# Second weights resident in SBUF, and a new hand-over to the second stretch of a mixture-of-experts kernel

## The chip, the cores and the metric

One core of one Trainium2 chip runs the whole program. The metric is the device time of one execution in microseconds (us). Engines are named TensorE (PE in the views; PEld is its weight load), VectorE (DVE), ScalarE (ACT), GpSimd (POOL) and SyncE (SP, which issues most DMA transfers).

## What is computed

Two transformer blocks with adaptive layer norm over 8 batches of 256 tokens of width 256. Block 0: causal softmax attention with 16 heads of 128, then a dense mixture of 8 experts (top 2). Block 1: linear attention, then a mixture of 16 experts of which each token takes 4. The change touches the last part and what runs beside it:

```python
    t = xf * rsqrt(mean(xf * xf) + EPS) * norm_w
    logits = t @ gate_w.T + gate_b
    vals, idx = top_k(logits, 4)
    gates_k = softmax(vals)
    G[m, idx] = gates_k
    h = einsum('mh,eoh->emo', t, w1) + b1
    a, b = minimum(h[..., ::2], 7.0), clip(h[..., 1::2], -7.0, 7.0)
    act = a * sigmoid(1.702 * a) * (b + 1.0)
    y = einsum('emi,edi->emd', act, w2) + b2
    delta = einsum('me,emd->md', G, y)
...
    x = x + gb * delta
```

## The kernel before

**Two tables of work.** Every engine runs its own list of stages. A planner (Plan.run, with a cost for each stage and a landing time for each transfer) merges chains of stages into these lists for the first part of the program. For the last part the lists are written by a loop by hand (lines 478 to 511). Semaphores hold every dependence, so the order alone is at stake.

**Routing and sending.** For batch b, f_gate gives the gate's logits, f_rank and f_pos the row of each (token, choice) in the DRAM tensor xsD, sorted by expert, and f_send scatters the tokens there: 8 indirect DMAs of 128 rows per batch on GpSimd (line 1905), all 8 on one semaphore of b % 4. f_gain and f_x (GpSimd, lines 1892 and 1897) make the batch's own output, which store writes to `out` (SyncE, line 840).

**Blocks.** 79 blocks of 128 sorted rows each belong to one expert; the expert's number stands in a table in SBUF (bi in the views), from which engines load it into a register. Block n runs through: xb (SyncE, line 810: its rows, 264 KB), w2x (SyncE, line 819: second weights of its expert, 256 KB, into a ring of four), w_in (ScalarE, line 1349: first weights, resident, times the norm's weight, two instructions), x_t and x_out (TensorE line 1073, ScalarE line 1356: rows transposed), h_mm (TensorE, line 1084: 8 calls, 16 instructions in the views), e_a, e_b, e_tanh, e_g, e_act (VectorE lines 1765, 1772, 1780, 1785, ScalarE line 1362: the gated activation), y_mm (TensorE, line 1093: 2 calls, 4 instructions), y_out (VectorE, line 1793) into a ring of five, YB: for n % 5 of 0, 1, 2 it shows as BC, 3 as RB, 4 as X, and tok and y_add (GpSimd, lines 1924 and 1934): an indirect DMA that adds the rows to `out` or, every second block, to accD. y_add n waits until y_add n-2 has landed. At the end merge (line 1941) adds accD to `out`.

**Two stretches.** Blocks 0 to 21 (FIRST = 22) hold the tokens of batches 0 to 4 and run beside the later batches; the planner sets their place. Blocks 22 to 78 hold the rest. Their rows can be loaded once every send of batch 7 has landed. Their xb ring has 11 places, and xb runs 8 blocks ahead. On SyncE they begin behind store 7 (lo is 22, ahead is 8, load_block adds xb n):

```python
    for n in range(lo, lo + ahead):
        load_block(n)
    for n in range(lo, lo + 2):
        p.add("w2x", n, slot=n % 4, by=16)
```

In the second stretch a turn of the loop puts on TensorE x_t n+1, h_mm n, y_mm n-2, and on ScalarE w_in n+1, x_out n+1, e_tanh n. The y product reads its weights from the ring W2 behind the wait for w2x:

```python
                on.wait_ge(*done("e_act", n))
                on.wait_ge(*done("w2x", n))
```

## Time and profile before

| | us |
|---|---|
| median of 3 runs | 1038.34 (1037.41 to 1038.93) |
| the profiled execution | 1038.5 |
| its span in the trace | 1036.2 |
| TensorE busy | 968.4 (93%) |
| VectorE busy | 725.9 (70%) |
| ScalarE busy | 673.3 (65%) |
| GpSimd busy | 427.6 (41%) |
| DMA traffic | 180.53 MB, mean 174 GB/s |
| granted TensorE clock, mean | 0.977 |

The profiled execution is one of the program; the page of its profile gives busy times and a chain of the work that ended last, of which TensorE holds 82%. The averages hide stages with different limits, so the rows below are read by stretch. An indirect DMA or a register load shows in a timeline on the engine that issues it; a bracket behind a row holds the idle time of that engine ahead of it and what ended it.

### The profile page before, as it was taken

The page shows a single profiled execution, that of the slowest core. Times are in us where ns is not written, and L with a number is a line of the kernel's source. Part 1 is how long each engine was busy: PE and PEld are TensorE (multiplying, and loading weights), DVE is VectorE, ACT ScalarE, POOL GpSimd, SP SyncE. Part 2 cuts the span into 40 slices and gives each one's busy share as a digit, 9 for nine tenths or more (in the row PEclk, how much of TensorE's full clock was granted, in tenths as well). Part 3 has the DMA queues.
Part 4 walks back from the last instruction along what each step waited for, and adds up shares of the span by engine and source line. Part 5 has one row for each costly group of instructions (what it writes and reads, how often), then busy time and mean ns, then how long its engine had stood idle before and what let it go on. Part 6 is the DMA issues. An engine that isn't in the chain of part 4 may idle for free.

```text
span 1036.2 us, 20508 instructions
## 1 busy us (share of the span) xinstructions
PE 968.4 (93%) x6020; PEld 821.6 (79%) x6020; DVE 725.9 (70%) x2545; ACT 673.3 (65%) x1944; POOL 427.6 (41%) x450
## 2 busy tenths in 40 slices
PE   7999999999999999999999999996879879999990
PEld 4769878888988887887888788885767769999980
DVE  3564656777767687777669677865888668888880
ACT  2657767668677767768767876782746347777650
POOL 3322421421461362255146136323165645666573
PEclk9999999999999999999999999998999899999995
DMA  9926992994799520020011004237268788899954
GB/s 307 306 84 223 375 375 88 338 377 145 278 358 379 179 84 1 22 94 22 1 67 70 2 12 163 66 133 277 53 163 185 203 221 217 223 226 225 227 120 81
DMA packets 93725, 180.53 MB, mean 174 GB/s; under 512 B 9949, under 2 KB 29085, under 8 KB 92717
## 3 DMA queue, kind: packets, MB, share of 16 engines
q1 hardware_dynamic: 73467, 148.55, 43.3%
q0 software_dynamic: 18800, 30.30, 13.1%
q8 instruction: 48, 0.79, 0.3%
q14 instruction: 64, 0.52, 0.2%
q10 hardware_dynamic: 1346, 0.36, 0.2%
HBM read 77.71 MB, written 107.99 MB: 179 GB/s over the span
## 4 chain that ended last, share of the span: by engine, by line
PE 82%; DVE 7%; issue 3%; DMA 2%; POOL 2%; ACT 1%; DVEq 0%; ACTq 0%; SPq 0%; POOLq 0%
PE bank L1084 12%; PE bank L1048 10%; PE bank L1020 10%; PE bank L1093 6%; PE bank L1038 5%; PE bank L1010 5%; PE bank L999 4%; PE bank L970 3%; PE bank L876 3%; PE bank L1039 2%; PE bank L885 2%; PE bank L1029 2%; PE bank L1009 2%; PE bank L954 2%; PE bank L992 2%
## 5 line engine op out<-in xcount | busy, mean ns | idle before, releaser
L1879 POOL TENSOR_TENSOR RB<-RB 128x512 f32<-128x512 f32 x64 | 66.7, 1042 | 277.3 <-DVE RB L1658 277.1
L1084 PE MATMUL bank<-RB 128*128 128x128 f32 x1264 | 158.1, 279 | 4.3 <-DVE BC L1772 1.7
L1084 PEld LDWEIGHTS bank<-RB 128*128 128x128 f32 x1264 | 151.3, 195 | 6.9 <-DVE BC L1772 2.3
L1349 ACT ACTIVATE RB<-RA,nw 128x512 f32 x158 | 105.4, 715 | 45.9 <-issue 18.7
L1048 PE MATMUL bank<-RA,RB 128*128 128x256 f32 x512 | 132.5, 381 | 0.3 <-issue 0.3
L1020 PE MATMUL bank<-RA 128*128 128x256 f32 x512 | 121.3, 380 | 0.0
L1020 PEld LDWEIGHTS bank<-RA 128*128 128x128 f32 x512 | 94.7, 190 | 15.0 <-issue 3.3
L1048 PEld LDWEIGHTS bank<-RA,RB 128*128 128x128 f32 x512 | 91.3, 190 | 13.6 <-issue 2.5
L1855 POOL TENSOR_TENSOR qs<-qs,half 128x4 f32<-128x4 f32 x64 | 65.6, 1025 | 63.6 <-DVE qs L1667 56.0
L1093 PE MATMUL bank<-RB,BC 128*128 128x256 f32 x316 | 83.7, 389 | 7.8 <-DVE BC L1785 7.0
L1250 ACT ACTIVATE RB<-bank 128x256 f32<-128x256 f32 x128 | 48.7, 380 | 45.7 <-PE bank L1039 43.1
L1038 PE MATMUL bank<-RB,RA 128*128 128x256 f32 x256 | 77.1, 383 | 0.0
L1905 POOL DMA_INDIRECT xsD<-SC,pu x64 | 65.7, 1026 | 27.2 <-issue 14.2
L1010 PE MATMUL bank<-RA 128*128 128x256 f32 x256 | 76.5, 380 | 0.0
L1658 DVE COPY RB<-bank 128x512 f32<-128x512 f32 x64 | 44.2, 690 | 44.3 <-PE bank L1020 43.9
L1231 ACT ACTIVATE RB<-bank 128x384 f32<-128x384 f32 x128 | 62.0, 490 | 20.1 <-PE bank L999 17.2
L1765 DVE TENSOR_SCALAR RB<-bank,b 128x128 f32<-128x128 f32 x158 | 48.1, 346 | 27.1 <-PE bank L1084 18.0
L1093 PEld LDWEIGHTS bank<-RB,BC 128*128 128x128 f32 x316 | 55.1, 194 | 14.6 <-DVE BC L1785 9.0
L1224 ACT ACTIVATE RB<-RB,sm 128x128 f32<-128x128 f32 x128 | 50.8, 397 | 23.4 <-DVE sm L1679 22.8
L1678 DVE CUSTOM_DVE_ANT_0 RB<-bank,cb,qs 128x128 f32<-128x128 f32 x128 | 44.1, 345 | 30.4 <-PE bank L1010 28.3
L1551 DVE SCALAR_TENSOR_TENSOR SC<-SC,bank 128x176 f32<-128x176 f32 x128 | 42.7, 333 | 30.9 <-ACT SC L1309 29.4
L1362 ACT ACTIVATE BC<-RB 128x256 f32<-128x256 f32 x79 | 32.8, 415 | 48.0 <-DVE RB L1765 43.3
(251 smaller groups left out, 2451.0 us busy)
## 6 DMA issues: line engine op xcount, KB each, us to landing
xsD<-BC SPq DMA_DIRECT2D x17, 4232.0 KB, 32.9
RB<-in_w2b SPq DMA_DIRECT2D x79, 256.0 KB
RB<-xsD SPq DMA_DIRECT2D x61, 264.5 KB
BC<-modD SPq DMA_DIRECT2D x16, 512.0 KB, 4.3
X<-xsD SPq DMA_DIRECT2D x18, 264.5 KB, 3.1
RA<-in_w SPq DMA_DIRECT2D x2, 2048.0 KB, 7.2
RA<-in_w SPq DMA_DIRECT2D x6, 512.0 KB, 8.7
RA<-in_L_attn_Wq SPq DMA_DIRECT2D x1, 2048.0 KB, 13.8
```

What stands on the lines that cost most here:

```text
L1010: pe.matmul(ps[:, 128:384], q[:, 128:256], k[:, 0:256], start=True, stop=True).then_inc(mine("scores", u), 1)
L1020: m = pe.matmul(psum("q_mm", p)[:, t * 256:t * 256 + 256], hT[:, b % 2, c, t * 128:t * 128 + 128], Wq[:, c, h * 128:h * 128 + 256], start= ...
L1038: pe.matmul(psum("pv", u)[:, 0:256], v[:, 0, :], PT[:, u % 2, 0:256], start=True, stop=False, skip_group_check=True)
L1048: m = pe.matmul(bank[5][:, t * 256:t * 256 + 256], OT[:, u % 2, t * 128:t * 128 + 128], Wo[:, h, :], start=(h == 0 and t == 0), stop=(h == ...
L1084: m = pe.matmul(ps[:, 128 * j:128 * j + 128], WS[:, n % 2, c, 128 * j:128 * j + 128], XT[:, n % 2, c * 128:c * 128 + 128], start=(c == 0), ...
L1093: m = pe.matmul(ps[:, 0:256], AB[:, n % 3, c * 128:c * 128 + 128], W2[:, n % 4, c, :], start=(c == 0), stop=(c == 1))
L1224: act.activation(P[:, u % 4, 0:128], P[:, u % 4, 0:128], ACT.Exp, bias=s[:, 2:3], scale=-1.0, accum_out=s[:, 4:5])
L1231: act.activation(PT[:, u % 2, :], psum("p_tout", u)[:, 0:384], ACT.Copy).then_inc(mine("p_tout", u), 1)
L1349: m = act.activation(WS[:, n % 2, c, :], W1[:, bass.ds(r, 1), c, :].rearrange("p a n -> p (a n)"), ACT.Copy, scale=nw[:, c:c + 1])
L1855: pool.tensor_tensor(dst, src, half[:, 0:n], ALU.pow).then_inc(sem, 1)
L1879: pool.tensor_tensor(sq, qrow, qrow, ALU.mult).then_inc(mine("q_sq", p), 1)
L1905: pool.indirect_dma_start(xsD[:, :], bass.IndirectOffsetOnAxis(pu[:, i, k:k + 1], 0), route(1)["src"][:, i, 0:ROW], None).then_inc(mine("f ...
```

## The change

All 16 second weights (4 MB) are loaded once into SBUF, W2R, in a region that layer 0 has left, by a new SyncE stage w2r, during batch 7 (the planner's tables get a cost of 1.0 and a landing of 3.0 for it). The y products of the second stretch take their weights from there by the expert's number, which TensorE loads into a register; their 57 w2x loads are gone. xb 22 and xb 23 are issued ahead of store 7, and x_t and x_out of blocks 22 and 23 are the planner's. y_mm 22 stands one turn earlier. The sends of batch 7 use three semaphores, and each waits for the send three back. Since the planner's list has new entries, its order around batch 7 moves as well.

```diff
-                yield do("f_send", 1, b, i, k, slot=b % 4, by=16, aside=(b > 3), after=[("f_gb", b), ("clear", 2 * b + 1)])
+                sent = 4 * i + k
+                three_back = [("f_send", 1, b, (sent - 3) // 4, (sent - 3) % 4)] * (b == NB - 1 and sent >= 3)
+                yield do("f_send", 1, b, i, k, slot=4 + sent % 3 if b == NB - 1 else b % 4, by=16, aside=(b > 3), after=[("f_gb", b), ("clear", 2 * b + 1)] + three_back)
...
+    def weights_stay():
+
+        for e in range(16):
+            after = [("s_x", NB - 1, 0), ("s_x", NB - 1, 1)] if e < 9 else [("wo1", NB - 1)] if e < 15 else [("n_bi", 1)]
+            yield do("w2r", e, by=16, aside=True, after=after + [("w2r", e - 2)] * (e >= 2))
+
+    def rest_begins():
+
+        for n in (FIRST, FIRST + 1):
+            yield do("xb", n, slot=RINGS[0] + (n - FIRST) % RINGS[1], by=16, aside=True, after=[("f_send", 1, NB - 1, 1, 3), ("n_bi", 1), ("wo1", NB - 1)])
+            p.chain(LATE, rest_turned(n))
+
+    def rest_turned(n):
+        yield do("x_t", n, bank=n % 2, first=True, after=[("xb", n), ("x_out", FIRST - 1)] + [("x_out", n - 1)])
+        yield do("x_out", n, bank=n % 2, last=True, after=[("h_mm", FIRST - 2 + n - FIRST)])
...
-    for steps in (weights_in(), weights_out(), block(0)):
+    for steps in (weights_in(), weights_out(), block(0), weights_stay()):
         p.chain(FILL, steps)
+    p.chain(LATE, rest_begins())
     p.run()
     lo, hi, ahead = FIRST, NBLK, 8
-    for n in range(lo, lo + ahead):
+    for n in range(lo + 2, lo + ahead):
         load_block(n)
-    for n in range(lo, lo + 2):
-        p.add("w2x", n, slot=n % 4, by=16)
...
-            p.add("x_t", n + 1, bank=bk, first=True)
+            if n > lo:
+                p.add("x_t", n + 1, bank=bk, first=True)
             p.add("w_in", n + 1)
-            p.add("x_out", n + 1, bank=bk, last=True)
+            if n > lo:
+                p.add("x_out", n + 1, bank=bk, last=True)
...
-        if lo <= n - 2 < hi:
+        if lo < n - 2 < hi:
             p.add("y_mm", n - 2, bank=5 + (n + 1) % 3, first=True)
-        if lo <= n and n + 2 < hi:
-            p.add("w2x", n + 2, slot=(n + 2) % 4, by=16)
+        if n == lo + 1:
+            p.add("y_mm", lo, bank=5 + lo % 3, first=True)
...
+        W2R = sc(0, 8192).rearrange("p (e c n) -> p e c n", e=16, c=2)
...
+            def w2r(e):
+
+                for t in range(2):
+                    on.wait_ge(*done("s_x", NB - 1, t))
+                if e >= 9:
+                    on.wait_ge(*done("wo1", NB - 1))
+                if e == 15:
+                    on.wait_ge(*done("n_bi", 1))
+                sp.dma_start(W2R[:, e, :, :].rearrange("p c n -> p (c n)"), I["w2b"][e]).then_inc(mine("w2r", e), 16)
...
                 on.wait_ge(*done("e_act", n))
-                on.wait_ge(*done("w2x", n))
+                if n < FIRST:
+                    on.wait_ge(*done("w2x", n))
+                    weights = [W2[:, n % 4, c, :] for c in range(2)]
+                else:
+                    on.wait_ge(*done("n_bi", 1))
+                    on.wait_ge(*done("w2r", 15))
+                    r = pe.value_load(table(0, n), min_val=0, max_val=15)
+                    weights = [W2R[:, bass.ds(r, 1), c, :].rearrange("p a n -> p (a n)") for c in range(2)]
                 clear("y_mm", n)
...
+                if b == NB - 1 and 4 * i + k >= 3:
+                    on.wait_ge(*done("f_send", l, b, (4 * i + k - 3) // 4, (k + 1) % 4))
```

ScalarE at the entry to the second stretch, before; L1356 is x_out (of block 22 the first here, of 23 the second), L1347 and L1349 are w_in, with its register load:

```order
L1347 TENSOR_LOAD bi
L1347 ISA x2
L1349 ISA
L1349 ACTIVATE RB<-RA,nw 128x512
L1349 ISA
L1349 ACTIVATE RB<-RA,nw 128x512
L1356 ACTIVATE RB<-bank0 128x256
L1347 TENSOR_LOAD bi
L1347 ISA x2
```

The same place after, where x_out is L1394 and w_in L1385 and L1387:

```order
L1394 ACTIVATE RB<-bank0 128x256
L1394 ACTIVATE RB<-bank1 128x256
L1385 TENSOR_LOAD bi
L1385 ISA x2
L1387 ISA
L1387 ACTIVATE RB<-RA,nw 128x512
L1387 ISA
L1387 ACTIVATE RB<-RA,nw 128x512
```

Before, w_in 22 stood ahead of x_out 22 and w_in 23 ahead of x_out 23; now both x_out stand ahead of both w_in.

TensorE from h_mm 23 on, before (x_t L1073, h_mm L1084, y_mm L1093): h_mm 23, x_t 25, h_mm 24, y_mm 22.

```order
L1084 MATMUL bank4<-RB 128x128 x8
L1073 MATMUL bank1<-ident,RB 128x128 x2
L1084 MATMUL bank2<-RB 128x128 x8
L1093 MATMUL bank6<-RB,BC 128x256 x2
L1073 MATMUL bank0<-ident,RB 128x128 x2
```

And after (x_t L1104, h_mm L1115, y_mm L1127 and L1131):

```order
L1115 MATMUL bank4<-RB 128x128 x8
L1127 TENSOR_LOAD bi
L1127 ISA x2
L1131 ISA
L1131 MATMUL bank6<-SC,BC 128x256
L1131 ISA
L1131 MATMUL bank6<-SC,BC 128x256
L1104 MATMUL bank1<-ident,RB 128x128 x2
L1115 MATMUL bank2<-RB 128x128 x8
```

y_mm 22 has moved from behind h_mm 24 to behind h_mm 23, and each y product of the second stretch has a register load ahead of it.

GpSimd around the sends of batch 7, before (sends L1905, y_add L1934, tok L1924, f_gain L1892, f_x L1897); the y_adds are those of blocks 15, 16, 17 and 18:

```order
L1905 DMA xsD<-SC,pu 34944x529 x8
L1934 DMA accD<-BC,to 2048x256
L1934 DMA out_0<-BC,to 2048x256
L1892 TENSOR_TENSOR SC<-SC,BC 128x512
L1924 COPY to<-RB 128x1
L1897 TENSOR_TENSOR X<-X,SC 128x512
L1934 DMA accD<-BC,to 2048x256
L1934 DMA out_0<-RB,to 2048x256
```

After (sends L1945, y_add L1974, tok L1964, f_gain L1930, f_x L1935):

```order
L1945 DMA xsD<-SC,pu 34944x529 x3
L1974 DMA accD<-BC,to 2048x256
L1945 DMA xsD<-SC,pu 34944x529 x3
L1974 DMA out_0<-BC,to 2048x256
L1945 DMA xsD<-SC,pu 34944x529 x2
L1974 DMA accD<-BC,to 2048x256
L1974 DMA out_0<-RB,to 2048x256
L1930 TENSOR_TENSOR SC<-SC,BC 128x512
L1964 COPY to<-RB 128x1
L1935 TENSOR_TENSOR X<-X,SC 128x512
```

The sends now have y_add 15 and y_add 16 among them, and f_gain and f_x have moved behind y_add 17 and y_add 18.

## Rows read from the trace of the kernel before

The first group's columns are the window, its length, the busy us of each engine (with instructions), the granted clock, the DMA engines' share and GB/s. A timeline's columns are the start in us, the length in us, engine, line, operation, tiles, count, and in brackets the idle time ahead.

**Rows 1.** windows view of four stretches, all engines:

```profile
812.00:824.00 12.00, 11.88 (x53) 9.98 (x54) 5.93 (x23) 2.96 (x7) 8.78 (x10) 0.57 0.71 226
824.00:834.00 10.00, 6.51 (x46) 5.53 (x44) 7.41 (x17) 3.64 (x8) 5.82 (x6) 1.00 0.67 148
834.00:846.00 12.00, 9.75 (x57) 8.58 (x58) 5.67 (x18) 4.33 (x9) 6.08 (x6) 0.86 0.99 256
...
900.00:950.00 50.00, 50.00 (x387) 47.42 (x386) 41.33 (x123) 35.29 (x70) 29.64 (x33) 1.00 0.93 224
```

**Rows 2.** timeline of GpSimd at the end (y_add 74, 75, 78, merge):

```profile
1007.53 1.71 POOL L1934 DMA_INDIRECT out<-X,to  x1 [0.16 <-issue]
...
1009.75 1.56 POOL L1934 DMA_INDIRECT accD<-BC,to  x1 [0.30 <-issue]
...
1015.47 1.55 POOL L1934 DMA_INDIRECT out<-RB,to  x1 [0.31 <-issue]
1018.77 0.95 POOL L1941 DMA_DIRECT2D out<-accD  x1 [1.75 <-DMA out<-RB,to]
```

**Rows 3.** timeline of VectorE: y_out of blocks 24, 69, 74 and 75:

```profile
860.40 0.49 DVE L1793 SCALAR_TENSOR_TENSOR X<-bank,RB 128x256 f32<-128x256 f32 x1
...
989.60 0.48 DVE L1793 SCALAR_TENSOR_TENSOR X<-bank,RB 128x256 f32<-128x256 f32 x1
...
1004.31 0.48 DVE L1793 SCALAR_TENSOR_TENSOR X<-bank,RB 128x256 f32<-128x256 f32 x1 [0.47 <-DMA accD<-BC,to]
...
1006.54 0.47 DVE L1793 SCALAR_TENSOR_TENSOR BC<-bank,RB 128x256 f32<-128x256 f32 x1
```

**Rows 4.** timeline of GpSimd: the y_add of blocks 24 and 69:

```profile
862.37 1.57 POOL L1934 DMA_INDIRECT out<-X,to  x1 [1.83 <-DVE BC L1785]
...
995.15 1.56 POOL L1934 DMA_INDIRECT accD<-X,to  x1 [0.39 <-POOL to L1924]
```

**Rows 5.** DMA issues of 850 to 1000 us, by kind:

```profile
RB<-in_w2b SPq DMA_DIRECT2D x52, 256.0 KB
```

**Rows 6.** source views: VectorE's register load; TensorE's semaphore wait:

```profile
L1752 DVEq TENSOR_LOAD <-bi x79: 299/305/784, 728.1 to 1003.1; - x79
L1752 DVEq FUSED_REGOPS  x79: 190/190/206, 728.7 to 1003.5; - x79
...
L78 PEldq EVENT_SEMAPHORE  x1: 51/51/51, 902.8 to 902.8; - x1
```

**Rows 7.** timeline of TensorE's weight loads at 902.5 to 905:

```profile
904.68 0.30 PEld L1093 LDWEIGHTS bank<-RB,BC 128*128 128x128 f32 x2
```

**Rows 8.** timeline of TensorE: h_mm is L1084, y_mm L1093, x_t L1073:

```profile
773.70 0.44 PE L1073 MATMUL bank<-ident,RB 128*128 128x128 f32 x2 [1.79 <-DMA RB<-xsD]
...
819.11 3.62 PE L1084 MATMUL bank<-RB 128*128 128x128 f32 x16
...
832.16 1.13 PE L1093 MATMUL bank<-RB,BC 128*128 128x256 f32 x4 [1.88 <-DVE BC L1785]
...
843.19 2.02 PE L1084 MATMUL bank<-RB 128*128 128x128 f32 x16 [0.35 <-issue]
...
848.38 2.02 PE L1084 MATMUL bank<-RB 128*128 128x128 f32 x16 [0.95 <-ACT RB L1356]
```

**Rows 9.** timeline of ScalarE: w_in 22 and x_out 22:

```profile
840.20 1.33 ACT L1349 ACTIVATE RB<-RA,nw 128x512 f32 x2 [0.23 <-issue]
842.66 0.38 ACT L1356 ACTIVATE RB<-bank 128x256 f32<-128x256 f32 x1 [1.13 <-PE bank L1073]
```

**Rows 10.** timeline of VectorE: e_g of block 18:

```profile
828.44 2.31 DVE L1780 SCALAR_TENSOR_TENSOR RB<-BC,RB 128x256 f32<-128x256 f32 x1 [0.61 <-ACT BC L1362]
```

**Rows 11.** timeline of GpSimd: f_gain of batch 7:

```profile
828.79 1.67 POOL L1892 TENSOR_TENSOR SC<-SC,BC 128x512 f32<-128x512 f32 x1
```

**Rows 12.** source view: the sends of batch 7:

```profile
L1905 POOL DMA_INDIRECT xsD<-SC,pu x8: 965/969/1214, 813.0 to 822.2; - x8
```

**Rows 13.** timeline of SyncE: xb 22 to 29, as one row:

```profile
833.16 8.14 SPq L810 DMA_DIRECT2D RB<-xsD  x8
```

## What the change will do, foretold

> **What bounds the kernel now.** Read the windows first [rows 1]. From 850 to 1000 us, most of the second stretch, TensorE is busy 50.00 of each 50 us at a granted clock of 1.00, in 387 instructions; a block has 22 (16 passes of h_mm, 4 of y_mm, 2 of x_t), so 17.6 blocks pass in 50 us, 2.84 us each. No transfer is waited for there, though the DMA engines are 0.93 busy. Hence 57 fewer weight loads gain nothing in this stretch: I cost that part at 0, and TensorE hides it. What can move the time lies at the two ends: the entry (812 to 850, where TensorE stands idle for 3.49 and 2.25 us in the second and third row, and where the first row has a clock of 0.57), and the tail after the last matmul.
>
> Next come the timelines of the tail. The last y product ends at about 1009, but the last y_add is issued at 1015.47, and the merge behind its landing at 1018.77 [rows 2]. From y_add 75 on GpSimd issues one every 1.91 us (1009.75 to 1015.47 is three steps), index copies between: it is the bound, because it began late. How late, the X tile tells, which only block n with n%5 = 4 writes [rows 3, 4]: block 24's y_out ends at 860.89 and its y_add starts at 862.37, 1.48 us later; block 69's end at 990.08 and 995.15, 5.07 us later. So y_add falls behind through the stretch. Each waits for the one two back to land; two per 5.3 us is about TensorE's pace, and a queue builds.
>
> **The change part by part.**
>
> (1) Weights on chip, tail. In the 150 us from 850 on, 52 loads of 256 KB are w2x [rows 5], 13.6 MB of what the DMA engines carry beside y_add. They go. If y_add then lands sooner, no queue is left: y_add 74 starts some 0.7 us after its y_out (ends 1004.79), at 1005.5, not 1007.53; y_add 75 waits for y_out 75 (1006.54 + 0.47 = 1007.01 [rows 3]) and starts at 1007.7; three steps of 1.91 give 1013.4 for y_add 78, not 1015.47: -2.05. y_out 74 besides waited 0.47 us for the landing of block 69's y_add, its ring slot; part of it comes off as well. I take **-2.2**. Bounds: 0 (the landing is set by y_add's own traffic) and -2.5.
>
> The rule that speaks against this gain is not about bytes but about queues, and the row is the DMA share of 0.93 at 850 to 1000. The Trainium skill, page "DMA: Bandwidth & Descriptors", section "Issuing engines are not separate DMA queues", says that transfers issued by different engines run on the same 16 DMA engines and interleave. By it SyncE's loads do slow GpSimd's y_add, and the sum is the one above; were they apart, this term would be 0. No row of before has y_add without loads in mid-stretch.
>
> (2) Weights on chip, the register. Each of the 57 y products now has TensorE load its expert's number into a register, behind the wait for e_act. TensorE does no such load before; the nearest rows are VectorE's: 0.305 us, and 0.19 us of register arithmetic [rows 6]; with the issue between and a check behind them I estimate 0.65 us. It hides if TensorE's sequencer runs ahead of the array. That shows in the same group: its wait for w2x is passed at 902.8, while that y product's first weights load at 904.68 [rows 7], with h_mm's 16 passes between. 1.8 us of cover against 0.65: 0 in steady state. The price without cover, 57 x 0.65 = 37 us, is a rival. Where e_act has only just ended (y_mm 22, 78) the 0.6 us show: y_mm 22 is counted in (4), and y_out 78 ended 6 us before its y_add, so there they hide.
>
> (3) 4 MB loaded in batch 7. The 16 transfers go into SyncE's order from behind xb 8 to behind xb 20, up to two ahead of a load that a block waits for. Nearest row: x_t 9 waits 1.79 us for its rows at 773.70 [rows 8]. The order of after puts y_mm 5 and h_mm 8 (2.9 us of TensorE) ahead of it, so that this wait can vanish (-1.8), while two weight loads, 512 KB at the 224 GB/s of [rows 1] = 2.3 us, can make those rows as much later. The gate chain of batch 7 (f_t, f_gate, f_rank) stands later, and x_out 14 behind another w_in (1.33 us [rows 9]). I take 0 for the sum, with -1.8 and +3 as ends.
>
> (4) Entry, ACT's order. Before, w_in 22 ran at 840.20 to 841.53 beside the wait for e_act 21, and h_mm 22 began at 843.19, 0.15 us after x_out 22 [rows 8, 9]. In after w_in 22 stands behind x_out 23. x_out 22 ends at 843.04, x_out 23 0.38 later (x_t 23 is done by then), then 0.25 us of register load and 1.33 of w_in: 845.0, and h_mm 22 at 845.15: +1.96. In return y_mm 22 is one h_mm sooner and stands where TensorE waited 0.95 us before h_mm 24: -0.95, but it waits itself for e_act 22 and its register, which I put at 0.75 (the 0.65 above and a hop). Net **+1.7**, bounds +1.0 (w_in 23 and 24 catch up) and +2.2.
>
> (5) Entry, f_gain and f_x of batch 7 later. Before, e_g of block 18 took 2.31 us [rows 10], where the same operation on the same shape takes 0.48 as y_out [rows 3], while f_gain ran on GpSimd from 828.79 [rows 11]; y_mm 18 then waited 1.88 us [rows 8]. In after f_gain stands behind y_add 18, which needs that very y_mm: it can't meet e_g 18. All after it is 1.9 us sooner, if f_gain then meets nothing: VectorE waits in most of the stretch that follows. I take **-1.9**; bounds -1.9 and 0 (it hits another e_g or e_act).
>
> The Trainium skill, page "SBUF — State Buffer", section "Who interferes with whom", gives a cause: a VectorE instruction with two SBUF inputs contends with a GpSimd instruction that reads SBUF. The two rows agree for e_g. By that rule e_a, e_b and y_out, with an input from PSUM, are safe and e_g and e_act are not, so the hit can come back; that is the second rival.
>
> (6) Sends on three semaphores, xb 22 and 23 ahead of store 7. Eight sends came from 813.0 to 822.2 [rows 12], one every 1.3 us. The send three back is 3.9 us old; the nearest landing in a row, the last y_add's, is within 3.3 us of its issue [rows 2], so that wait holds nothing up. The last two now stand behind y_add 16 (y_out 16 sets that, about 827), so they land near 833, and xb 22 is asked for about when it was, 833.16 [rows 13]; x_t 22 wants its rows shortly before 843.19 [rows 8], 1.9 us sooner after (5). Cost 0: hidden behind blocks 18 to 21. Store 7 and xb 24 to 29 come some 7 us later, xb 24 near 841 for an x_t at 845: just hidden.
>
> **Sum.** -2.2 + 0 + 0 + 1.7 - 1.9 + 0 = -2.4 us. The profiled execution took 1038.5 (span 1036.2 and 2.3 around it), so 1036.1; on the median of 1038.34 that is 1035.9. I write 1036.0.
>
> **The rivals.** 0.2%, 2.1 us, is about what a measurement of this kernel can tell from no change.
>
> A. *The gains are there, but in the wrong place* (the change doesn't do what it says). Either y_add's landing stays, set by its own descriptors, or f_gain hits the next e_g. For: VectorE does an e_g and an e_act in every block. Against: y_add's gap to y_out shrinks from 5.07 us (block 69) to 2.74 (block 74) once loads run out at 1001. It gives -2.4 + 1.9 = -0.5, or -2.4 + 2.2 = -0.2: about 1038.0.
>
> B. *Slower: the longer wait at the entry takes the clock down.* [rows 1] show what idle time does here: after waits the clock is 0.57 in 812 to 824, and h_mm 18 takes 3.62 us, where h_mm 22 takes 2.02 [rows 8]; it is 0.86 in 834 to 846. After this change TensorE waits 2.3 us ahead of h_mm 22 and 0.75 ahead of y_mm 22, close together, behind a wait for e_act 21. Two h_mm at such a clock cost 2 x 1.6 = +3.2; with (5) lost too, 1.7 - 2.2 + 3.2 = +2.7: 1041.0. It decides from the point where the clock falls during h_mm 22 or 23; before, h_mm 22's 2.02 us say that it did not.
>
> C. *Slower by far: the register load drains TensorE.* 57 x 0.65 = +37: about 1073. Against it stands that VectorE's and ACT's own loads run beside their busy work.
>
> D. *Better: x_t 9's wait gone and no clock fall in 812 to 824.* -2.4 - 1.8 = -4.2, and with h_mm 18 at the full clock (-1.6) -5.8: 1034.1 to 1032.5. For: x_t 17 to 19 and the gate matmuls are spread in another order, and the planner keeps TensorE's next work ready. Against: the gate chain comes later.
>
> **How the numbers follow.** Forecast 0.40, A 0.26, B (with late weights or gate chain in batch 7, (3)'s +3, which ends near 1039 to 1041 too) 0.19, C 0.04, D 0.11. The forecast's -2.4 lies close to the bound, so 0.25 of its 0.40 is faster, 0.14 the same, 0.01 slower; A is 0.20 the same, 0.04 faster and 0.02 slower; B is 0.17 slower and 0.02 the same; D is faster. Faster 0.40, same 0.36, slower 0.24. The range 1031.5 to 1041.5 holds D, with the term bounds on that side, and most of B; it leaves out C and some of each end. The forecast's own is 1034 to 1038.
>
> **What would show it.** In the profile of after: TensorE still 50.00 of 50 from 860 on, no TensorE idle time released by a register load there, and a block still 2.84 us (else C). DMA throughput at 850 to 1000 down from 224 to some 130 GB/s; the X tile's y_add 1 to 2 us behind its y_out at every n, the last y_add under 4 us behind the last y_out (else A). h_mm 22 2.1 us or more behind x_out 22's end. e_g 18 at 0.41 us; where f_gain stands, an e_g or e_act of over 1 us would be A. A granted clock below 1.00 in the 10 us from h_mm 22 would be B. The prediction is wrong if the stretch from 760 to 812, which I put at 0, moves by more than 2 us.

## The result and the profile after

The changed kernel takes 1039.49 us (median of 22 runs), the kernel before 1037.43 (22 runs). The ratio is 1.0023, 95% interval 1.0015 to 1.0030: 2.1 to 2.4 us slower, where 2.4 us faster was forecast. The profiled executions alone would say the opposite, 1037.8 us (span 1035.5) after and 1038.5 before: after's lies 1.7 us below its kernel's median and before's 1.1 above its own. Executions of one kernel differ by some 3 us either way, and the longer ones have the lower mean clock (after's seven above 1041 us 0.974 to 0.978, its other fifteen 0.978 to 0.985), so the profiles below are read for mechanisms and the times for sizes. One of the twelve executions of e3, a kernel below, took 2053.74 us and is left out of its numbers.

The windows of the kernel after, with the columns of [rows 1]:

```profile
812.00:824.00 12.00, 10.18 (x73) 8.15 (x72) 9.20 (x40) 4.30 (x9) 8.68 (x9) 1.00 0.76 213
824.00:834.00 10.00, 8.64 (x59) 7.31 (x57) 7.90 (x26) 4.76 (x10) 7.42 (x7) 1.00 0.79 214
834.00:846.00 12.00, 6.66 (x41) 5.79 (x42) 5.20 (x10) 3.74 (x7) 8.31 (x11) 0.86 0.90 225
900.00:950.00 50.00, 50.00 (x387) 47.42 (x386) 41.28 (x123) 35.34 (x71) 30.68 (x36) 1.00 0.71 137
```

The second stretch is as before: 50.00 of 50 busy, 387 instructions. The DMA rate has fallen from 224 to 137 GB/s. The first row's clock is 1.00 instead of 0.57, and the second has 1.36 us of idle time instead of 3.49; the third has 5.34 instead of 2.25. Each profile is one execution: where a clock falls in it can differ in the next.

Timeline of VectorE, y_out (now L1831) of blocks 69, 74 and 75, which answers [rows 3], and then of GpSimd, y_add 69, 74 to 78 (L1974) and merge (L1981), which answers [rows 2, 4]:

```profile
989.22 0.48 DVE L1831 SCALAR_TENSOR_TENSOR X<-bank,RB 128x256 f32<-128x256 f32 x1
...
1003.94 0.48 DVE L1831 SCALAR_TENSOR_TENSOR X<-bank,RB 128x256 f32<-128x256 f32 x1 [0.47 <-issue]
...
1006.17 0.47 DVE L1831 SCALAR_TENSOR_TENSOR BC<-bank,RB 128x256 f32<-128x256 f32 x1
```

```profile
990.48 1.56 POOL L1974 DMA_INDIRECT accD<-X,to  x1 [1.09 <-DVE RB L1818]
...
1005.21 1.57 POOL L1974 DMA_INDIRECT out<-X,to  x1 [1.48 <-DVE BC L1823]
...
1007.49 1.56 POOL L1974 DMA_INDIRECT accD<-BC,to  x1 [0.49 <-DVE BC L1823]
...
1009.42 1.57 POOL L1974 DMA_INDIRECT out<-BC,to  x1 [0.16 <-issue]
...
1012.31 1.56 POOL L1974 DMA_INDIRECT accD<-BC,to  x1 [1.12 <-DMA out<-BC,to]
1014.17 1.55 POOL L1974 DMA_INDIRECT out<-RB,to  x1 [0.30 <-issue]
1017.46 2.58 POOL L1981 DMA_DIRECT2D out<-accD  x3 [1.74 <-DMA out<-RB,to]
```

Block 69's y_out ends at 989.70 and its y_add starts at 990.48, 0.78 us later instead of 5.07. The queue is gone, y_add 75 starts 0.85 us behind its y_out, y_add 76 at the pace of 1.93. But y_add 77 then waits 1.12 us for the landing of a y_add, which it had not done before, and y_add 78 still starts 4.04 us behind the end of its y_out. Measured from h_mm 78, the merge starts 14.56 us later (1002.90 to 1017.46) and before 15.51 (1003.26 to 1018.77): the tail gives 0.95 us. The profiles of the runs below agree: this distance is 14.05 to 15.00 us in the fifteen profiles with resident weights (median 14.3) and 15.1 to 15.8 in the four with a w2x ring of four (median 15.4), so the tail is worth about 1.2 us.

The register load of the y products (TensorE's queue) and the DMA totals of 850 to 1000 us, which answer [rows 6] and [rows 5]:

```profile
L1127 PEldq TENSOR_LOAD <-bi x57: 296/301/494, 846.5 to 1007.5; - x57
L1127 PEldq FUSED_REGOPS  x57: 151/151/165, 847.0 to 1008.0; - x57
```

```profile
DMA packets 13885, 18.30 MB, mean 122 GB/s; under 512 B 2572, under 2 KB 7948, under 8 KB 13862
```

0.301 and 0.151 us for each of 57 loads, and none of it shows in the windows row of 900 to 950. Before, the same stretch moved 32.24 MB.

Ahead of the entry one wait is new. TensorE (x_t L1104, h_mm L1115) and ScalarE (w_in L1387, x_out L1394, and L1298, the squares of batch 7's norm) at block 14:

```profile
796.69 0.38 PE L1104 MATMUL bank<-ident,RB 128*128 128x128 f32 x2
...
800.01 2.02 PE L1115 MATMUL bank<-RB 128*128 128x128 f32 x16 [1.66 <-ACT RB L1394]
```

```profile
797.52 1.33 ACT L1387 ACTIVATE RB<-RA,nw 128x512 f32 x2 [1.31 <-PE bank L1104]
798.76 0.40 ACT L1298 ACTIVATE SC<-SC 128x256 f32<-128x256 f32 x1
...
799.55 0.36 ACT L1394 ACTIVATE RB<-bank 128x256 f32<-128x256 f32 x1
```

x_t 14 has ended at 797.07, but the planner's new order has put w_in 15 and those squares ahead of x_out 14, and h_mm 14 waits 1.66 us for it. Before, x_out 14 stood ahead of w_in 15 and h_mm 14 (798.16) waited for nothing:

```profile
795.02 0.36 ACT L1356 ACTIVATE RB<-bank 128x256 f32<-128x256 f32 x1
...
797.13 1.33 ACT L1349 ACTIVATE RB<-RA,nw 128x512 f32 x2 [0.23 <-issue]
```

The entry: TensorE (x_t is L1104, h_mm L1115, y_mm L1131), ScalarE (x_out L1394, w_in L1387), VectorE (y_out L1831, e_g L1818, e_act L1823) and GpSimd (f_gain L1930, f_x L1935), which answer [rows 8 to 11]; last SyncE's xb 22 and 23, for [rows 13]:

```profile
774.68 0.44 PE L1104 MATMUL bank<-ident,RB 128*128 128x128 f32 x2
...
830.80 1.95 PE L1115 MATMUL bank<-RB 128*128 128x128 f32 x16
...
837.28 2.07 PE L1131 MATMUL bank<-RB,BC 128*128 128x256 f32 x4 [3.67 <-DVE BC L1823]
...
842.27 2.05 PE L1115 MATMUL bank<-RB 128*128 128x128 f32 x16 [2.06 <-ACT RB L1387]
...
847.45 1.13 PE L1131 MATMUL bank<-SC,BC 128*128 x4 [1.13 <-DVE RB L1803]
```

```profile
839.82 0.81 ACT L1394 ACTIVATE RB<-bank 128x256 f32<-128x256 f32 x2 [5.87 <-PE bank L1104]
840.89 2.56 ACT L1387 ACTIVATE RB<-RA,nw 128x512 f32 x4 [0.25 <-issue]
```

```profile
833.93 0.48 DVE L1831 SCALAR_TENSOR_TENSOR BC<-bank,X 128x256 f32<-128x256 f32 x1
834.33 1.54 DVE L1818 SCALAR_TENSOR_TENSOR RB<-BC,RB 128x256 f32<-128x256 f32 x1
835.90 1.33 DVE L1823 SCALAR_TENSOR_TENSOR BC<-BC,RB 128x256 f32<-128x256 f32 x1
```

```profile
833.91 1.67 POOL L1930 TENSOR_TENSOR SC<-SC,BC 128x512 f32<-128x512 f32 x1
...
835.66 1.28 POOL L1935 TENSOR_TENSOR X<-X,SC 128x512 f32<-128x512 f32 x1
```

```profile
834.09 1.43 SPq L831 DMA_DIRECT2D RB<-xsD  x2
```

Of before, h_mm 21, and e_g and e_act 21:

```profile
836.13 2.64 PE L1084 MATMUL bank<-RB 128*128 128x128 f32 x16
```

```profile
840.35 0.42 DVE L1780 SCALAR_TENSOR_TENSOR RB<-BC,RB 128x256 f32<-128x256 f32 x1
...
840.79 0.42 DVE L1785 SCALAR_TENSOR_TENSOR BC<-BC,RB 128x256 f32<-128x256 f32 x1
```

h_mm 21 begins at 830.80, 5.3 us sooner than before (836.13). Then the lead goes: h_mm 22 begins at 842.27, only 0.92 us sooner than in [rows 8]. From one to the other it is 11.47 us instead of 7.06. Three rows hold all of the 4.4 us between: e_g and e_act 21 take 1.54 and 1.33 us beside f_gain and f_x (+2.0), y_mm 21 takes 2.07 and not 1.13 (+0.9, clock 0.86), and h_mm 22 waits 2.06 us for w_in 22, which stands behind both x_out (+1.7); that is 4.6, and other steps give 0.2 back.

### The profile page after: what moved, and what is told of

The parts are those of the page before. It is cut to its first block, busy times and chain, and to the rows that moved or that the text cites. A ratio compares the mean times of both kernels' runs of the same rounds, so it can differ in the third digit from the quotient of the medians.

```text
span 1035.5 us, 20408 instructions
## 1 busy us (share of the span) xinstructions
PE 964.7 (93%) x6020; PEld 816.7 (79%) x6020; DVE 725.3 (70%) x2545; ACT 673.5 (65%) x1944; POOL 426.3 (41%) x450
## 4 chain that ended last, share of the span: by engine, by line
PE 81%; DVE 7%; issue 3%; DMA 2%; POOL 2%; ACT 1%; SPq 1%; another core or an unknown queue 1%; ACTq 0%; DVEq 0%; POOLq 0%
PE bank L1115 12%; PE bank L1079 10%; PE bank L1051 10%; PE bank L1131 5%; PE bank L1069 5%; PE bank L1041 5%; PE bank L1030 4%; PE bank L1001 3%; PE bank L907 3%; PE bank L1070 2%; PE bank L916 2%; PE bank L1060 2%; PE bank L1040 2%; PE bank L985 2%; PE bank L1023 2%
## 5 line engine op out<-in xcount | busy, mean ns | idle before, releaser
L1115 PE MATMUL bank<-RB 128*128 128x128 f32 x1264 | 154.8, 276 | 7.3 <-ACT RB L1387 3.2
L1115 PEld LDWEIGHTS bank<-RB 128*128 128x128 f32 x1264 | 147.9, 192 | 10.7 <-ACT RB L1387 4.2
L1387 ACT ACTIVATE RB<-RA,nw 128x512 f32 x158 | 105.3, 715 | 43.8 <-issue 17.1
L1945 POOL DMA_INDIRECT xsD<-SC,pu x64 | 65.5, 1023 | 27.8 <-DVE pu L1632 14.3
L1269 ACT ACTIVATE RB<-bank 128x384 f32<-128x384 f32 x128 | 62.1, 490 | 20.1 <-PE bank L1030 17.2
L1803 DVE TENSOR_SCALAR RB<-bank,b 128x128 f32<-128x128 f32 x158 | 48.0, 346 | 28.8 <-PE bank L1115 21.4
L1282 ACT ACTIVATE RB<-RB,sm 128x256 f32<-128x256 f32 x128 | 63.8, 498 | 0.0
L1263 ACT ACTIVATE RB<-RB,sm 128x256 f32<-128x256 f32 x128 | 63.6, 497 | 0.0
```

The lines of the kernel that those rows point to most:

```text
L1115: m = pe.matmul(ps[:, 128 * j:128 * j + 128], WS[:, n % 2, c, 128 * j:128 * j + 128], XT[:, n % 2, c * 128:c * 128 + 128], start=(c == 0), ...
L1263: act.activation(P[:, u % 4, 128:384], P[:, u % 4, 128:384], ACT.Exp, bias=s[:, 3:4], scale=-1.0, accum_out=s[:, 5:6]).then_inc(mine("s_ex ...
L1269: act.activation(PT[:, u % 2, :], psum("p_tout", u)[:, 0:384], ACT.Copy).then_inc(mine("p_tout", u), 1)
L1282: act.activation(P[:, u % 4, 128:384], P[:, u % 4, 128:384], ACT.Copy, scale=s[:, 7:8]).then_inc(mine("p_norm", u), 1)
L1387: m = act.activation(WS[:, n % 2, c, :], W1[:, bass.ds(r, 1), c, :].rearrange("p a n -> p (a n)"), ACT.Copy, scale=nw[:, c:c + 1])
L1945: pool.indirect_dma_start(xsD[:, :], bass.IndirectOffsetOnAxis(pu[:, i, k:k + 1], 0), route(1)["src"][:, i, 0:ROW], None).then_inc(mine("f ...
```

## The experiments

Each kernel was timed with before on the same chip; ratios are to that before, with 95% intervals, and 0.001 is 1.04 us. Differences below are taken from the ratios; the quotient of two medians lies up to 0.0012 away from them. Chips differ: before takes 1037.7 to 1038.4 us on the chips of e1 to e4 (called chip 7), e5 to e8 (chip 6) and e13 to e16 (chip 12), and 1029.8 to 1031.3 on that of e9 to e12, e17 and e18 (chip 11). Kernels are compared within one chip where that was done, and it is said where not.

### Resident weights and the rest apart (e1, e2)

e1 is before with w2r, the register load and no w2x from block 22 on; e2 is after without them (w2x 22 and 23 ahead of xb 24):

```diff
-    for steps in (weights_in(), weights_out(), block(0), weights_stay()):
+    for steps in (weights_in(), weights_out(), block(0)):
...
+    for n in range(lo, lo + 2):
+        p.add("w2x", n, slot=n % 4, by=16)
     for n in range(lo + 2, lo + ahead):
```

> The kernel before with the second weights resident and nothing else of the change: w2r in batch 7, y_mm of the second stretch by register, no w2x after block 21; sends, xb 22 ahead, x_out ahead of w_in and y_mm 22's place are as before. The planner moves batch 7's work by itself, since w2r is in its list. Theory 1 (the loss sits at the hand-over: w_in 22 behind x_out 23, f_gain and f_x beside e_g and e_act 21): this kernel has the tail's -1.3 to -2.3 us and none of that loss, so 1.5 to 2.5 us below before. Theory 2 (the loss sits in batch 7: 4 MB more and the gate chain 3 to 5 us later, so that xb 22 comes late): at or above the kernel after, +2 us on before. Both: TensorE still 50.00 of 50 from 860 on.

> The kernel after without the resident weights: w2x from the ring for all blocks, w2x 22 and 23 issued ahead of xb 24; xb 22 and 23 ahead of store 7, x_out ahead of w_in, y_mm 22 sooner and the sends on three semaphores stay. Theory 1: the entry's loss (w_in 22 about +2 us, f_gain and f_x up to +2) without the tail's gain: +2 to +4 us on before. Theory 2: within 1 us of before. The last y_add again 5 us or more behind the last y_out, as in the kernel before, by both.

Measured: e1 1037.28 us, 1.0000 (0.9988 to 1.0012); e2 1037.59 us, 1.0002 (0.9991 to 1.0013). Neither theory had both right: each half is level with before, and the whole is 2.1 us above it. Without w2r the planner leaves most of batch 7 in before's order, so e2 also shows that the new order comes with w2r: in e1's profile h_mm 14 waits for x_out 14 as in after (1.67 us), in e2's it does not.

### w_in ahead of x_out (e3), f_gain later (e4), both (e8)

```diff
     p.add("merge", by=16 * 4)
+    p = p.moved([("w_in", lo), ("w_in", lo + 1)], ("e_tanh", lo - 1))
```

In e4 it is ("f_gain", 7) and ("f_x", 7), moved behind ("y_add", 20), and xb 24 to 27 behind xb 23; e8 has both edits. moved puts the named stages behind another one and counts the semaphores anew.

> The kernel after with w_in 22 and 23 ahead of x_out 22 on ScalarE, nothing else moved. In the profile of after ScalarE waits 5.9 us before x_out 22 and then h_mm 22 waits 2.06 us for w_in 22. Theory 1: -2.0 us on the kernel after (h_mm 22 within 0.2 us of x_out 22's end), so at or just below before. Theory 2: -2.0 too if xb 22 is there in time; 0 if xb 22 lands last. If the clock (rival B) is what the longer wait costs, more than 2: -3 to -4.

> The kernel after with f_gain and f_x of batch 7 behind y_add 20 on GpSimd, and xb 24 to 27 ahead of store 7 on SyncE so that they don't wait for it. In the profile of after e_g 21 took 1.54 and e_act 21 1.33 us beside f_gain (833.91) and f_x (835.66), where 0.41 is usual. Theory 1: e_g and e_act 21 back to 0.41, y_mm 21 2.0 us sooner; h_mm 22 follows if xb 22 has landed by then: -2.0 on the kernel after. Theory 2 (xb 22, issued at 834.09 and wanted now at 837, is late): less than 0.5 us.

> The kernel e3_w_in_first with f_gain and f_x of batch 7 behind y_add 20 (and xb 24 to 27 ahead of store 7). In e3's profile e_g 21 took 0.88 and e_act 21 1.34 us beside them, and h_mm 22 began 0.2 us behind x_out 22. Theory 1: y_mm 21 1.4 us sooner and h_mm 22 with it, -1.4 on e3. Theory 2: x_t 22 stands behind y_mm 21 on TensorE and its rows, asked for at 835.2, land at 839 or so: not sooner, 0.

Measured: e3 1.0002 (0.9991 to 1.0014), 2.2 us below after's 1.0023 (other chips), as theory 1 had it. TensorE in e3, h_mm 22:

```profile
840.32 2.02 PE L1129 MATMUL bank<-RB 128*128 128x128 f32 x16 [0.23 <-ACT RB L1408]
```

The wait ahead of it is 0.23 us instead of 2.06. e4 came to 1.0008 (0.9996 to 1.0021), 1.6 us below after, and e8 to 0.9988 (0.9975 to 1.0000), 1.5 us below e3 (each time another chip); the intervals overlap, so a gain from f_gain's place is likely and not settled. Its mechanism shows: VectorE in e4, e_g and e_act 21:

```profile
840.80 0.41 DVE L1833 SCALAR_TENSOR_TENSOR RB<-BC,RB 128x256 f32<-128x256 f32 x1
841.25 0.42 DVE L1838 SCALAR_TENSOR_TENSOR BC<-BC,RB 128x256 f32<-128x256 f32 x1
```

The other profiles show how general it is. In all sixteen profiles where f_gain is not moved behind y_add 20, it and f_x meet an e_g or e_act of block 18, 20 or 21, which then takes 0.88 to 2.63 us instead of 0.41. Of the four where it is moved (e4, e8, e11, e17) e4 has no such row, and the others have one, e_g 22 at 0.88 to 0.94 us.

### w_in behind x_out alone in before (e14)

```diff
     p.add("merge", by=16 * 4)
+    p = p.moved([("w_in", lo)], ("x_out", lo + 1))
+    p = p.moved([("w_in", lo + 1)], ("w_in", lo))
```

> The kernel before with one thing of the change: w_in 22 and w_in 23 behind x_out 23 on ScalarE. All else word for word as before. Place-of-w_in theory: h_mm 22 about 1.9 us behind x_out 22's end instead of 0.15, and +1.0 to +1.9 us on before (some comes back in the wait before h_mm 24). If x_t 22's rows or the clock set the entry anyway: 0.

Measured: 1039.62 us, 1.0020 (1.0008 to 1.0032): +2.1 us, with 0.8 to 3.3 as its interval (1.2 by the medians). TensorE, h_mm 22, and ScalarE, both x_out (L1371) and w_in 22 and 23 (L1364):

```profile
843.29 2.05 PE L1099 MATMUL bank<-RB 128*128 128x128 f32 x16 [2.06 <-issue]
```

```profile
841.04 0.66 ACT L1371 ACTIVATE RB<-bank 128x256 f32<-128x256 f32 x2 [2.69 <-PE bank L1088]
841.90 2.56 ACT L1364 ACTIVATE RB<-RA,nw 128x512 f32 x4 [0.20 <-issue]
```

One swap on ScalarE is about as large as the whole loss of after. h_mm 22 waits 2.06 us; both x_out end at 841.70, and it begins 1.59 us behind them, where in before it began 0.15 us behind x_out 22.

### The order of batch 7 (e5, e6, e9, e10, e16, e18)

e5 is e2 with w_in first. e6 is e5 with resident weights, but w2r is put into SyncE's finished list instead of the planner's, behind the same loads as in after, so that no other engine's order moves:

```diff
-    for steps in (weights_in(), weights_out(), block(0), weights_stay()):
+    for steps in (weights_in(), weights_out(), block(0)):
...
+    places = {("xb", 8): (0, 1), ("w2x", 8): (2, 3), ("xb", 9): (4, 5), ("xb", 10): (6,), ("w2x", 11): (7, 8),
+              ("w2x", 13): (9, 10), ("xb", 14): (11, 12), ("xb", 15): (13, 14), ("xb", 20): (15,)}
```

e9 does the same to before (against e1); e10 is e6 with w_in behind x_out. e16 is e6 again, beside after (e13) and e14 on one chip, and e18 is e10 beside e17.

> The kernel e2_rest_only (all of the change but the resident weights) with w_in 22 and 23 ahead of x_out 22. Resident weights alone and the rest alone each came out level with before, both together 2.1 us above it, and w_in first took 2.1 us off the kernel after. Theory 2 (w2r and the order it brings to batch 7 cost 2 to 3 us, the tail gives 1.2 back): without w2r the -2.1 of w_in first come on top of e2's 0, so 2 us below before (1035.5) and below e3_w_in_first. Theory 1 alone (all loss at the hand-over, batch 7 free): resident weights are a gain of 1.2, so this is 1 us above e3, near 1038.3.

> The kernel e5_rest_w_in_first with the second weights resident, but the order of ScalarE, VectorE, GpSimd and TensorE in batch 7 kept as in e5: w2r stands on SyncE behind the same loads as in the kernel after. Against e5 it tells the price of the 4 MB with the register loads; against e3 (same but for the planner's own order) the price of the order. If the traffic costs (loads of rows land 1 to 2 us later in batch 7): +1 to +2 on e5. If the order alone did it: -1.2 on e5 (the tail).

> The kernel before, order of every engine word for word kept, with w2r put into SyncE's list behind the same loads as in the kernel after, no w2x after block 21, and the register load before each y_mm of the second stretch. It prices resident weights alone, without the new order that the planner made of batch 7. Tail gain as measured (merge 1.0 to 1.4 us less behind h_mm 78), traffic 0 to +1: 0.5 to 1.4 us below before. e1 (the same with the planner's new order) was level with before, so if the order costs, this is 1 us or more below e1; if not, it is level too.

> The kernel after with the order of batch 7 as the planner makes it without w2r (w2r put behind the same loads); w_in 22 stays behind x_out 23. Order theory: the new order is worth 2 us of after's +2.1, so this is level with before (1037.7). Hand-over theory (w_in 22 is the 2.1 us, the order nothing): it stays near the kernel after, +1.5 to +2 on before.

> The kernel after, unchanged, on the chip of the next three, as their base. +2 us on before by every theory; +3.5 or more, as e10 and e12 had on another chip, if the loss depends on the chip.

> The kernel e6 (resident weights, the change's sends and xb 22, batch 7's order kept, w_in 22 and 23 first) beside after on one chip. By e6 (0.9978) 4 us below e13 and 2 below before; by e11 on another chip (1.0007, the same with f_gain late) 3 below e13 and level with before.

> The kernel e10 (e16 with w_in 22 and 23 behind x_out 23, which is the kernel after with batch 7's order kept). Place of w_in worth 2.1 us, as e14 measured it: 0.999 of before, 2.1 above e16, and 2 to 2.5 us below the kernel after, which would be the price of the new order. If e10's 1.0035 stands: the place of w_in is worth 6 us here and the order nothing in after.

Of these seven kernels only e5 has no resident weights:

| kernel | batch 7's order | w_in 22, 23 | chip | us | ratio to before |
|---|---|---|---|---|---|
| e5 | old | first | 6 | 1036.83 | 0.9994 (0.9982 to 1.0006) |
| e6 | old | first | 6 | 1035.58 | 0.9978 (0.9966 to 0.9990) |
| e9 (before's sends and entry) | old | first | 11 | 1028.12 | 0.9983 (0.9971 to 0.9995) |
| e10 | old | behind | 11 | 1032.45 | 1.0035 (1.0020 to 1.0050) |
| e13 (after) | new | behind | 12 | 1039.19 | 1.0014 (1.0001 to 1.0027) |
| e16 (e6 again) | old | first | 12 | 1035.31 | 0.9970 (0.9958 to 0.9982) |
| e18 (e10 again) | old | behind | 11 | 1033.64 | 1.0020 (1.0005 to 1.0036) |

Resident weights in before's own order gain 1.8 us (e9); with the planner's order nothing (e1, another chip). e6 is 1.7 us below e5 on one chip, so the 4 MB loaded in batch 7 cost no more than the tail gives. On one chip, e13 to e16 is 4.6 us (3.9 by the medians). If w_in's place is worth e14's 2.1 us there, the other 2.5 are the order; e3 against e6 (chips apart) says 2.5 too. That is a remainder: no two kernels that differ in the order alone were timed on one chip. e16 beats both kernels: 3.1 us below before, 4.6 below after.

The profiles say where a part of it lies. From h_mm 9 to h_mm 14 the kernels without w2r take 19.1 to 19.3 us, those with w2r in the old order 19.8 to 20.1, and those with the new order 20.7 to 21.4 (e1, e10 and e16, which have a clock fall inside this stretch, are left out). So here the loads cost 0.7 to 1.0 us and the order about 1 more. The wait of h_mm 14 for x_out 14, 1.58 to 1.68 us, is in all eight profiles with the new order (after, e1, e3, e4, e8, e12, e13, e15) and in none of the other twelve. No run puts x_out 14 alone back ahead of w_in 15.

One finding disagrees. e10 and e18, with the order kept and w_in behind, should stand at 0.9991 to 0.9999 by that sum (e16 and e6 with 2.1 us added), and stand at 1.0035 and 1.0020, on the chip where before is 8 us faster. There is a kernel that was run on both chips and answers a part of this: e12 and e15, below, are the same kernel, at 1.0046 (1.0028 to 1.0064) on chip 11 and 1.0011 (1.0000 to 1.0021) on chip 12. So that kernel stands 0.0035 higher against before on chip 11; if the same holds for e10 and e18, they come to 1.0000 and 0.9985 with that taken off, on either side of what the sum has. Within chip 11 the order is e12 against e10, 1.1 us, and against e18, 2.7 us, if the useless matmuls of e12 are worth nothing; the intervals overlap. Why chip 11 is different is not shown. One profile has a hint: in e9's, with before's order, h_mm 21 begins at 826.27, 9 to 10 us sooner than in before (836.13) and e14 (835.20), and f_gain meets the e_g of another block. A before that loses less there leaves less for the change to win.

e10's profile also has a clock fall; its windows and TensorE's y_mm 21 and h_mm 22:

```profile
818.00:828.00 10.00, 8.80 (x62) 7.67 (x61) 7.25 (x24) 3.19 (x8) 8.17 (x8) 1.00 0.82 236
828.00:840.00 12.00, 6.88 (x26) 6.01 (x27) 3.48 (x6) 3.50 (x7) 8.08 (x11) 0.59 0.91 232
```

```profile
831.06 2.07 PE L1158 MATMUL bank<-RB,BC 128*128 128x256 f32 x4 [3.23 <-DVE BC L1850]
...
836.05 3.79 PE L1142 MATMUL bank<-RB 128*128 128x128 f32 x16 [2.06 <-ACT RB L1414]
```

Behind waits of 3.23 and 2.06 us the granted clock is 0.59 in 828 to 840, and h_mm 22 takes 3.79 us instead of 1.95 to 2.05. e18, the same kernel, has no such fall in its profile (h_mm 22 at 2.05 us).

### The clock (e12, e15)

```diff
             def y_mm(n):
                 ps = psum("y_mm", n)
+                if n == FIRST - 1:
+                    clear("y_mm", n)
+                    for i in range(12):
+                        pe.matmul(ps[:, 0:128], ident[:, :], ident[:, :], start=True, stop=True)
                 on.wait_ge(*done("e_act", n))
```

and the same with 8 products in h_mm, for n == FIRST, ahead of its waits. e15 is this kernel again, beside after.

> The kernel after with useless matmuls in TensorE's two waits at the entry, 12 products of the identity with itself ahead of y_mm 21's wait (2.7 us of 3.7) and 8 ahead of h_mm 22's (1.8 us of 2.1), into the banks that y_mm 21 and h_mm 22 then overwrite. Clock theory (rival B: the longer wait takes the clock down in a part of the executions; 7 of 22 of the kernel after took over 1041 at a mean clock of 0.974 to 0.978): those go, y_mm 21 takes 1.1 and not 2.1 us, and the median falls by 1 to 2 us. Otherwise 0 to +0.3.

> The kernel e12 (after with useless matmuls in the two waits at the entry), now beside after on one chip. Clock theory: 1 to 2 us below e13. Otherwise level with e13.

Measured: e12 1.0046 (1.0028 to 1.0064), without after on its chip; e15 1.0011 (1.0000 to 1.0021) beside e13's 1.0014. The last two windows, 834 to 850, of e13 and then of e15:

```profile
834.00:846.00 12.00, 6.60 (x23) 4.69 (x22) 4.90 (x9) 3.75 (x7) 8.86 (x11) 0.60 0.87 219
846.00:850.00 4.00, 4.00 (x21) 4.00 (x21) 1.55 (x6) 0.72 (x2) 0.00 (x0) 0.50 0.95 281
```

```profile
834.00:846.00 12.00, 11.22 (x88) 10.17 (x87) 4.86 (x12) 3.75 (x7) 9.30 (x12) 1.00 0.86 201
846.00:850.00 4.00, 2.85 (x22) 2.51 (x21) 3.59 (x12) 3.38 (x7) 0.52 (x3) 1.00 0.95 257
```

e13's profiled execution has rival B in full: clock 0.60 and 0.50, h_mm 22 at 3.78 us and h_mm 23 at 2.74, together 2.6 us over 1.95. e15's has 1.00 throughout. Yet the two ratios are 0.3 us apart, within their intervals, and the two medians 0.4 the other way. The useless matmuls did act on the clock beyond the one profile: the mean granted clock of e15's executions is 0.981 in the median, of e13's 0.978. The falls are real and cost what they show, but no gain of time from keeping TensorE busy in two waits is seen; one of 1 us would be hard to tell with these intervals. Against rival B as the cause of the loss there is a second number: over all its 22 executions after's mean clock is 0.979 in the median, and before's is 0.979 on each of the chips 6, 7 and 12. The falls are not tied to the wait for w_in either: in the profiled executions of e5, e6 and e9, where w_in 22 is first, h_mm 22 took 3.35, 3.14 and 3.02 us, and of the seven kernels with a wait of 2.06 us ahead of h_mm 22 four show it (e2, e4, e10, e13: 2.70 to 3.79 us) and three do not (after, e14, e18: 2.05). What sets them off in one execution and not in another is open.

### Loads asked for sooner, instead of resident (e7), and the last pair (e11, e17)

e7 is e5 with a ring of 16 for w2x, asked for further and further ahead:

```diff
-        if lo <= n and n + 2 < hi:
-            p.add("w2x", n + 2, slot=(n + 2) % 4, by=16)
+        if lo <= n:
+            while asked < min(hi, n + 3 + (n - lo) // 4):
+                p.add("w2x", asked, slot=4 + asked % 16, by=16)
+                asked += 1
```

> The kernel e5 with a ring of 16 for the second stretch's w2x, in the region of W2R, and w2x asked for 2 to 13 blocks ahead (one more every four blocks), so that the loads end some 12 blocks before the last block; no register load on TensorE, nothing added to batch 7. If y_add's lag is set by loads that run beside it, the tail is 1 to 1.4 us shorter than e5's, as in the kernel after, and the time 1 us below e5: about 1034.5, below both kernels. If the extra loads (240 GB/s instead of 215) hold up rows or y_add in mid-stretch, it is level with e5 or above.

Measured: 1037.82 us, 0.9998 (0.9984 to 1.0011), level with e5 (0.4 us above it by the ratios, 1.0 by the medians). DMA totals of 850 to 900 us, and the last two y_adds (L1994):

```profile
DMA packets 7800, 12.27 MB, mean 245 GB/s; under 512 B 1115, under 2 KB 2738, under 8 KB 7791
```

```profile
1012.65 1.57 POOL L1994 DMA_INDIRECT accD<-BC,to  x1 [0.63 <-issue]
1014.52 1.55 POOL L1994 DMA_INDIRECT out<-RB,to  x1 [0.30 <-issue]
```

At 245 GB/s (before, in these 50 us: 213) the y_adds fell behind further. The X tile's y_add starts 8.84 us behind its y_out at block 59 (4.71 in before, 1.03 in after) and still 4.00 at block 74 (2.74 and 0.78), and y_add 78 starts 13.7 us behind h_mm 78 (1000.86), in e5 12.5, in before 12.2 and in after 11.3. So the lag grew with the rate while blocks ran, and the last 12 blocks without w2x did not clear it; this is one execution.

e11 is e6 with f_gain late; e17 is e11 again, beside e18.

> The kernel e6_old_order (resident weights, order kept, w_in first; 0.9978 of before) with f_gain and f_x of batch 7 behind y_add 20 and xb 24 to 27 ahead of store 7, which took 1.4 us off e3 in e8. Expected -1 on e6: 1034.6, or 0 if y_mm 21 then waits for something else. It should beat both kernels by 2 to 3.5 us.

> The kernel e11 (e16 with f_gain and f_x of batch 7 behind y_add 20) on another chip than e11's. If the chip made the difference to e16: 0.997 of before or below. If f_gain late costs in this order: 1.000 or above again.

Measured: 1.0007 (0.9995 to 1.0020) and 1.0000 (0.9986 to 1.0013), against 0.9978 and 0.9970 for e6 and e16 without that move. e17 was to run on another chip than e11 and ran on the same one, chip 11, so it could not tell its two theories apart. The chip is the likelier reason: the 0.0035 by which chip 11 sets e12 above e15 is about what e11 and e17 stand above e6 and e16 (0.0029 and 0.0030). And e17 to e18, on one chip, differ by w_in's place and f_gain's, 2.1 us: if w_in's place is worth 2.1, f_gain late costs nothing there, and gains nothing.

## Why the prediction was wrong

The time lay in the range and the sign was wrong: two terms, (5) and (3), failed, and (1) was half its size. By the steps:

(1) The tail, -2.2: right mechanism, too large. The X tile's lag went from 5.07 to 0.78 us, as said, and y_add 74 to 76 came at the forecast distances. The term counted three steps of 1.91 us behind y_add 75; one of them had a wait of 1.12 us for a landing in it, and the last y_add stood 4.04 us behind the last y_out, not under 4. Measured: 0.95 in the profile, about 1.2 over all profiles, and 1.8 by e9's time, where resident weights are the only change. That y_add lands sooner once SyncE's loads are gone is also what the rule of the Trainium skill cited there would have (page "DMA: Bandwidth & Descriptors", section "Issuing engines are not separate DMA queues"): the lag of 0.78 us agrees with it, and e7, with more loads, from the other side. (The share of 0.93 that I gave for 850 to 1000 us is the row of 900 to 950; over the whole stretch it is 0.89, at 215 GB/s.)

(2) The register load, 0: right. The sequencer ran ahead, TensorE stayed at 50.00 of 50, rival C did not happen. At y_mm 22, 847.45, it stood 1.0 us behind e_act 22 (846.44), where I had put 0.75.

(3) Resident weights' cost in batch 7, 0: this step failed. I named its parts, among them "x_out 14 behind another w_in", and let them cancel without a size. Measured, h_mm 8 was 1.95 us sooner and x_t 9's wait gone, but h_mm 9 stood level again (779.11 against 779.01); then h_mm 14 waited 1.66 us for x_out 14 and stood 1.85 us later. The stretch from h_mm 9 to h_mm 14 takes 1.7 us more than before, of which the loads are 0.7 to 1.0 by the kernels in the old order. By the times the whole order may cost more, 2.5 us as a remainder (e13, e14, e16); where the rest of that would lie, and whether f_t's 4.9 us of delay has a part in it, is not shown.

(4) w_in behind x_out, +1.7 net: the mechanism was right and the size close. e14 alone gives +2.1 (0.8 to 3.3); I took 0.2 off because y_mm 22 comes sooner, and after lost that again: y_mm 22 waited 1.13 us itself.

(5) f_gain and f_x later, -1.9: the step that failed most. e_g 18 was back at 0.41 us and TensorE was 5.3 us ahead at h_mm 21, more than forecast. But f_gain (833.91) and f_x (835.66) met e_g and e_act 21, the last two steps ahead of y_mm 21, at 1.54 and 1.33 us, 2.0 us more than without them, and gave the 1.9 back at once. That is rival A. The condition that I wrote, "if f_gain then meets nothing", was the whole term, and VectorE's idle time that I relied on had moved with the rest; the sixteen profiles with such a meeting say that to meet nothing would have been the exception. The rule of the Trainium skill, page "SBUF — State Buffer", section "Who interferes with whom", held in both halves: y_out 20 at 833.93, one input in PSUM, took 0.48 us beside f_gain. So the trace agrees that the next two-input instruction pays.

(6) The sends and xb 22, 0: right for what it asked. xb 22 was asked for at 834.09 (before 833.16), and in after h_mm 22 waited for w_in, not for rows. With w_in first the rows do come last: in e8's profile x_t 23 waits 0.80 us for them. As a time the change without resident weights and with w_in first is worth -0.6 us (e5, interval -1.9 to +0.6).

The sum by the runs is -1.0 to -1.8 (resident weights), +2.1 (w_in, e14), about +2.5 (order, the remainder) and -0.6 to -1.9 for the rest (e5's 0.9994; e2's 1.0002 less w_in's 2.1), together +0.9 to +3.0. With only what the profiles locate, -1.2 (tail), +1.7 (h_mm 9 to 14), +2.1 and the same -0.6 to -1.9, it is +0.7 to +2.0. Measured are 2.1 to 2.4 and 1.5 in e13, so neither sum is excluded. Rival B, the clock, is in e13's profile at nearly the price foretold (2.6 us against 3.2), but e15 and the mean clock of all executions do not bear it out as the cause of the median.

## What to carry to other kernels

When a planner sets an order, new entries reorder work that the diff never names: put the new work into the old order first, and time that apart from the new order. Work that is ready and was done inside a wait (w_in 22) must stay ahead of the instruction that ends the wait, and work for a later block (w_in 15) must not come between that instruction and the one that releases it (x_out 14). A slow neighbour that is moved off one instruction lands on another: look up what runs beside its new place after everything else has moved too, and give the term no size before that.

## What the runs showed of the hardware

Chips differ by 0.8%: before takes 1029.8 to 1031.3 us on one and 1037.7 to 1038.4 on others. A ratio to before does not carry over between them either: one and the same kernel stood at 1.0046 on the faster chip (e12) and 1.0011 on another (e15), intervals apart. In after's tail the y_add of 1012.31 still waited for the landing of an earlier one, with DMA traffic of 8 GB/s over 1000 to 1020. And filling TensorE's waits with useless matmuls held the clock at 1.00 in 834 to 850 in e15's profile and raised the mean clock of its executions from 0.978 to 0.981, without a gain of time that can be seen.
